# Eight first tiles of the final stage loaded in the expert stage, and eight more tiles kept on chip, in a three-stage graph kernel

## The chip, the cores and the metric

The kernel runs on one core of a Trainium2 chip. The metric is the time of one launch on the device in microseconds (us), measured on the chip. TensorE does the matrix products, VectorE, ScalarE and GpSimd the elementwise work, SyncE (SP) issues most of the DMA transfers; ScalarE (ACT in the rows) issues the stores of the result. GpSimd is POOL in the rows, VectorE DVE, TensorE PE, with PEld for its loads of weights. A q behind a name (SPq, POOLq) is the engine's queue, which works off waits, registers and branches.

## The reference, cut to what matters

There are 128 graphs of 128 nodes with 512 features each; x and adj are drawn at random.

```python
x = layernorm(x + attention(x, adj, adj, Wq, Wk, Wv, Wo))     # 16 heads, bias 2 * adj
# mixture of experts on the graph
scores = x.mean(axis=1) @ router_w + router_b
top1 = argmax(scores)                                          # one of 4 experts for each graph
out = einsum('bnm,bmk->bnk', adj, einsum('bnh,bhk->bnk', x, expert_w[top1]))
s, ss = sums of out and of out * out over the nodes and the graphs of each expert
y = (out - mean[top1]) * rsqrt(var[top1] + 1e-5) * gamma[top1] + beta[top1]
x = layernorm(x + relu(y))
```

The statistics of an expert need `out` of all its graphs, so `y` can be made only when the last `out` is there.

## The kernel before

One tile is one graph: 128 nodes on the partitions and 512 features in fp32, 262,144 bytes. The kernel has three stages, with a meeting of all engines between two of them.

The attention stage makes `x1`, the first normalised result, tile by tile and stores it to `x1_dram` (`x_scratch` in the rows). Its working tiles lie in `kept`, an array of 32 tiles in the chip's SBUF memory that the next stage fills.

The expert stage (`expert_phase`) takes 128 steps of one tile. SP loads x1 and the transposed adjacency four steps ahead into rings of four (`g_x1`, called `x1` in the function and `g_x` in the rows, and `adj_t`). TensorE forms adj @ x1 two steps ahead and then the product with the chosen expert's weights, each product as three passes over high and low parts. ScalarE copies the result (L752) and squares it (L754), and GpSimd adds both into the expert's sums (L835, L839). Every fourth tile (`is_kept`, place 2 of 4) is copied to `kept` and stays on chip. The other 96 go to a ring `g_out` and are stored by SP to `y_dram` (`y_scratch`, L663). The loop's body is written out for 8 steps and runs 15 times; the last 8 steps are written out after it with constants. Steps of such a written-out round are called peeled below.

The final stage (`norm_phase`) first makes the coefficients of each expert from the sums (TensorE, VectorE, ScalarE; `mul_row` is the last of them that GpSimd waits for, L1047). Then 128 steps follow in rings of 16 places: GpSimd multiplies the y tile with the expert's row (`scale`, L1101 to L1111), four tiles ahead of the rest; TensorE adds the expert's second row; VectorE takes the relu, adds x1 in place (L1058) and collects statistics; for every four tiles (a quad) GpSimd makes `rstd` (L1124) and `nb` (L1126); ScalarE applies them (L1144) and issues the store of the result (L1147). Before each scaling GpSimd's queue reads the number of the tile's expert into a register (L1102).

SP's queue sets the order of the loads. It first fills the ring of 16 (12 y tiles and 16 x1 tiles). In the loop it goes through the places in order: the y tile of the next round once TensorE has used the old one (L922), then the x1 tile once the old one's result has been stored (L925). y and x1 of a place count on one semaphore, so GpSimd's wait for a tile that isn't kept is a wait for both loads:

```python
                if is_kept(s):
                    pool.wait_ge(z_done, t + 1)
                    src = kept[:, bass.ds(i * QUADS + s // UNROLL, 1), :].rearrange("p a n -> p (a n)")
                else:
                    pool.wait_ge(tiles_in[s], i * 32 + 32)
                    src = y[:, s]
```

## Time and profile before

| What | Value |
|---|---|
| Median of three runs | 2771.8 us |
| Lowest and highest run | 2770.59 and 2773.67 us |
| The profiled execution's own time | 2769.72 us |
| Its span, first to last instruction | 2768.0 us |
| Busy share TensorE, VectorE, ScalarE, GpSimd | 96%, 69%, 55%, 46% |
| Attention, expert and final stage | to about 1985, to 2507, to 2768 us of the span |

The busy shares are means over three stages with different limits, so they tell little of the final stage. There one reads the stretches by themselves: how busy the DMA engines are in each, what an engine waits for there, and the distance from one quad to the next. A DMA share of 1.05 means all 16 DMA engines busy all the time.

### The profile page before, as it was taken

To read this page: it belongs to the slowest core of one execution; us is meant where nothing else is said; L and a number is where in the kernel's file an instruction comes from. 1 tells how busy PE (TensorE), PEld (TensorE's weight loads), DVE (VectorE), ACT (ScalarE), POOL (GpSimd) and SP (SyncE) were. 2 spreads that over 40 slices of the span, in tenths; PEclk is the share of its full clock that TensorE was granted. 3 is DMA by queue.
4 is the path that set the end of the run, shared out by engine and by line. 5 is a ranking of instruction groups with operands and counts; after the bars stand their busy time and mean duration, and the time that the engine had idled before them with its cause. 6 is when DMAs were issued, how large, how long until landed. Compare 5 with 4: busy or idle time off the path is not lost. (4 is left out here: it accounts for less than half of the span.)

```text
span 2768.0 us, 77846 instructions
## 1 busy us (share of the span) xinstructions
PE 2662.7 (96%) x22583; PEld 2264.7 (82%) x22584; DVE 1918.4 (69%) x8351; ACT 1514.5 (55%) x5391; POOL 1282.0 (46%) x1174
## 2 busy tenths in 40 slices
PE   8999999999999999999999999999799999997776
PEld 7898989898989888888888888888688888883232
DVE  6777777777777777777777777777733333335887
ACT  5565666666665656565656565656544444442444
POOL 2333334343434333334333433343366666666887
PEclk9999999999999999999999999999899999998998
DMA  4111111111111111111111111111234344445999
GB/s 147 62 53 54 53 62 53 54 53 62 53 54 53 62 54 53 57 58 58 49 58 56 58 49 64 51 57 52 75 123 141 131 138 131 136 134 197 396 405 352
DMA packets 169427, 277.32 MB, mean 100 GB/s; under 512 B 19378, under 2 KB 52146, under 8 KB 168882
## 3 DMA queue, kind: packets, MB, share of 16 engines
q1 hardware_dynamic: 150962, 243.36, 26.2%
q10 hardware_dynamic: 18432, 33.56, 3.2%
q8 instruction: 15, 0.25, 0.0%
q14 instruction: 18, 0.15, 0.0%
HBM read 184.57 MB, written 92.27 MB: 100 GB/s over the span
## 5 line engine op out<-in xcount | busy, mean ns | idle before, releaser
L553 POOL TENSOR_TENSOR kept<-kept,row_scale 128x512 f32<-128x512 f32 x512 | 533.4, 1042 | 1106.5 <-DVE row_scale L437 1096.4
L331 ACT ACTIVATE kept<-kept,neg_max 128x128 f32<-128x128 f32 x2048 | 796.0, 397 | 138.0 <-DVE neg_max L413 138.0
L413 DVE CUSTOM_DVE_ANT_0 kept<-att_bank,adj_nat 128x128 f32<-128x128 f32 x2048 | 442.6, 286 | 3.6 <-PE att_bank L212 1.6
L331 ACT ACTIVATION_READ_ACCUMULATOR kept<-kept,neg_max 128x1 f32 x2048 | 399.9, 195 | 0.0
L422 DVE TENSOR_REDUCE abs_max<-kept 128x4 f32<-128x512 f32 x512 | 349.2, 682 | 0.1
L191 PE MATMUL att_bank<-xt_hi,w_hi 128*128 128x256 f32 x2048 | 329.2, 283 | 11.2 <-DVE w_lo L390 11.2
L191 PE MATMUL att_bank<-xt_hi,w_lo 128*128 128x256 f32 x2048 | 329.7, 283 | 0.0
L191 PE MATMUL att_bank<-xt_lo,w_hi 128*128 128x256 f32 x2048 | 329.1, 283 | 0.0
L191 PEld LDWEIGHTS att_bank<-xt_hi,w_hi 128*128 128x128 f32 x2048 | 298.7, 191 | 30.7 <-issue 10.8
L364 ACT ACTIVATE kept<-att_bank 128x512 f32<-128x512 f32 x256 | 153.2, 599 | 279.8 <-PE att_bank L250 279.6
L191 PEld LDWEIGHTS att_bank<-xt_hi,w_lo 128*128 128x128 f32 x2048 | 282.7, 191 | 0.0
L191 PEld LDWEIGHTS att_bank<-xt_lo,w_hi 128*128 128x128 f32 x2048 | 282.4, 191 | 0.0
L479 DVE TENSOR_TENSOR o_lo<-att_bank,o_hi 128x512 fp32r<-128x512 f32 x128 | 88.5, 692 | 248.7 <-ACT o_hi L367 248.7
L250 PE MATMUL att_bank<-ident,kept 128*128 128x128 f32 x2048 | 248.1, 274 | 6.4 <-POOL kept L553 6.3
L463 DVE COPY kept<-att_bank 128x512 f32<-128x512 f32 x256 | 176.0, 688 | 94.9 <-PE att_bank L250 94.9
L250 PEld LDWEIGHTS att_bank<-ident,kept 128*128 128x128 f32 x2048 | 227.8, 141 | 9.1 <-POOL kept L553 5.4
L546 POOL TENSOR_TENSOR xt_lo<-kept,xt_hi 128x1024 fp32r<-128x1024 f32 x64 | 151.5, 2368 | 126.8 <-DVE xt_hi L475 117.0
L367 ACT ACTIVATE o_hi<-att_bank 128x512 fp32r<-128x512 f32 x128 | 76.5, 597 | 233.8 <-PE att_bank L258 233.8
L989 PE MATMUL ps_z<-n_y,ident 128*128 128x512 f32 x256 | 151.7, 676 | 52.3 <-POOL n_y L1109 47.5
L835 POOL TENSOR_TENSOR out_sum<-out_sum,g_out 128x512 f32 x96 | 123.7, 1289 | 134.9 <-ACT g_out L752 134.9
L1144 ACT ACTIVATE n_x<-n_x,n_nb,n_rstd 128x512 f32<-128x512 f32 x128 | 104.4, 815 | 131.3 <-POOL n_nb L1126 78.9
L752 ACT ACTIVATE g_out<-ps_o 128x512 f32<-128x512 f32 x96 | 57.4, 598 | 217.0 <-PE ps_o L702 217.0
(136 smaller groups left out, 5233.4 us busy)
## 6 DMA issues: line engine op xcount, KB each, us to landing
kept<-in_x_t SPq DMA_DIRECT2D x64, 512.0 KB, 3.5
kept<-in_x SPq DMA_DIRECT2D x128, 256.0 KB, 2.5
x_scratch<-kept SPq DMA_DIRECT2D x128, 256.0 KB, 2.0
g_x<-x_scratch SPq DMA_DIRECT2D x128, 256.0 KB, 2.7
n_x<-x_scratch SPq DMA_DIRECT2D x128, 256.0 KB, 6.2
out_x<-n_x ACTq DMA_DIRECT2D x128, 256.0 KB, 5.4
y_scratch<-g_out SPq DMA_DIRECT2D x96, 256.0 KB, 2.0
n_y<-y_scratch SPq DMA_DIRECT2D x96, 256.0 KB, 5.6
```

Source lines behind the costliest of these rows:

```text
L191: mm = pe.matmul(dst, w[:, which, k, c * P:(c + 1) * P], x[:, par, k, :], start=m == 0, stop=m == len(todo) - 1)
L250: mm = pe.transpose(bank[c][:, r * P:(r + 1) * P], probs[:, h * P:(h + 1) * P], ident[:, :])
L331: nc.scalar.activation(probs[:, h * P:(h + 1) * P], neg_s[:, h * P:(h + 1) * P], ACT.Exp, bias=neg_max[:, h:h + 1], scale=-1.0, accum_out= ...
L364: nc.scalar.activation(probs_t[:, c * D:(c + 1) * D], bank[c][:, :], ACT.Copy).then_inc(pt_odd, 1)
L413: nc.vector.tensor_tensor_reduce(neg_s[:, h * P:(h + 1) * P], bank[r][:, c * P:(c + 1) * P], adj_nat[:, s], -2.0, BIG, ALU.add, ALU.min, n ...
L422: nc.vector.tensor_reduce(abs_max[:, heads], neg_s[:, c * D:(c + 1) * D].rearrange("p (h m) -> p h m", h=HC), AX_X, ALU.max, apply_absolut ...
L463: nc.vector.tensor_copy(probs_t[:, c * D:(c + 1) * D], bank[c][:, :]).then_inc(pt_even, 1)
L546: nc.gpsimd.tensor_tensor(xt_lo[:, p], xt_stage[:, p], xt_hi[:, p].bitcast(F32), ALU.subtract).then_inc(xt_lo_done, 1)
L553: nc.gpsimd.tensor_tensor(part, part, by, ALU.mult).then_inc(probs_done, 1)
L835: nc.gpsimd.tensor_tensor(acc, acc, src, ALU.add).then_inc(sum_done, 1)
L989: pe.matmul(dst, ident[:, :], y[:, s], start=True, stop=False)
L1144: nc.scalar.activation(x1[:, s], x1[:, s], ACT.Identity, bias=nb[:, u, k:k + 1], scale=rstd[:, u, k:k + 1]).then_inc(out_done, 1)
```

## The change

Three things are changed together.

First, the first eight x1 tiles of the final stage are loaded while the expert stage ends: tiles 0 to 3 in steps 120 to 123 into a new array `early`, tiles 4 to 7 in steps 124 to 127 into the expert stage's ring `g_x1`, whose places are free by then. The two arrays become places 0 to 7 of the final stage's x1 ring (`x1_of`); places 8 to 15 remain in an array of their own.

Second, place 15 of every 16 tiles is kept too. Its eight tiles go to `w_stage`, the array through which weights were staged, so 88 instead of 96 tiles are stored and loaded again.

Third, to tell place 15 of 16 apart, the expert stage's loop body is written out for 16 steps and runs 7 times, with 16 peeled steps behind it. To make room, `g_out` has three places instead of four, the rows of `adj_t` are shorter, and the adjacency tiles and some small columns of the attention stage move into `kept`.

```diff
 BIG = 3.0e38
 UNROLL = 4
 KEPT_EVERY = UNROLL
+SPAN = 4 * UNROLL
+EARLY = 2 * UNROLL
 GROUP = 2
...
 def is_kept(s):
-    return s % KEPT_EVERY == KEPT_EVERY - 2
+    return s % KEPT_EVERY == KEPT_EVERY - 2 or s % SPAN == SPAN - 1
+
+
+def kept_tile(kept, more_kept, s, quad, span):
+
+    if s % SPAN == SPAN - 1:
+        return more_kept[:, bass.ds(span, 1), :].rearrange("p a n -> p (a n)")
+    return kept[:, bass.ds(quad, 1), :].rearrange("p a n -> p (a n)")
 def attention_phase(nc, io, W_hi, W_lo, w_stage, expert_w_in, ident, ones, g_x1, adj_t, hand_over, kept, pair,
...
         qk = [half[:, :, :].rearrange("p (w a) (b n) -> p w (a b) n", w=2, n=GN) for half in pair]
         xt_hi = sb("xt_hi", [P, 2, C, GN], F32R)
         xt_lo = sb("xt_lo", [P, 2, C, GN], F32R)
-        adj_nat = sb("adj_nat", [P, UNROLL, P])
+        adj_nat = kept[:, 30].rearrange("p (u n) -> p u n", u=UNROLL)
         o_hi = sb("o_hi", [P, C, P], F32R)
         o_lo = sb("o_lo", [P, C, P], F32R)
-        neg_max = sb("neg_max", [P, HEADS])
-        row_sum = sb("row_sum", [P, HEADS])
-        abs_max = sb("abs_max", [P, HEADS])
-        inv_sum = sb("inv_sum", [P, HEADS])
-        row_scale = sb("row_scale", [P, HEADS])
+        neg_max = kept[:, 31, 0 * HEADS:1 * HEADS]
+        row_sum = kept[:, 31, 1 * HEADS:2 * HEADS]
+        abs_max = kept[:, 31, 2 * HEADS:3 * HEADS]
+        inv_sum = kept[:, 31, 3 * HEADS:4 * HEADS]
+        row_scale = kept[:, 31, 4 * HEADS:5 * HEADS]
         stats = sb("stats", [P, 2, 6])
         mean_var = sb("mean_var", [P, 2, 2])
         var_eps = sb("var_eps", [P, 2])
...
     C = D // P
     HALF = C // 2
-    ROUNDS = 2
+    ROUNDS = SPAN // UNROLL
     with ExitStack() as ctx:
         def sb(name, shape, dt=F32):
             return ctx.enter_context(nc.sbuf_tensor(name, shape, dt))
...
         scores = sb("scores", [1, 2, 8])
         best = sb("best", [1, 2, 8])
         best_at = sb("best_at", [1, 2, 8], U32)
-        out = sb("g_out", [P, UNROLL, D])
+        out = sb("g_out", [P, UNROLL - 1, D])
         sq = sb("g_sq", [P, 2, D])
         ps_y = [ctx.enter_context(nc.psum_tensor(f"ps_y{i}", [P, 2, D], F32)) for i in range(2)]
...
                 for n in range(ROUNDS):
                     for s in range(UNROLL):
                         r = i * ROUNDS + n
-                        body(r * UNROLL + s, s, r, last, (n, s) == (ROUNDS - 1, UNROLL - 1))
+                        body(r * UNROLL + s, s, r, last, n * UNROLL + s, i)
             with eng.Fori(0, B // (ROUNDS * UNROLL) - 1) as i:
                 rounds(i, False)
             rounds(B // (ROUNDS * UNROLL) - 1, True)
+
+        def stores_ahead(s, place, span):
+
+            a_span = sum(not is_kept(n * UNROLL + s) for n in range(ROUNDS))
+            return span * a_span + sum(not is_kept(n * UNROLL + s) for n in range(place // UNROLL))
+
+        def out_of(s):
+            return out[:, s if s < KEPT_EVERY - 2 else s - 1]
         def exists(step, last, ahead):
             return not last or step + ahead < B
...
             sp.dma_start(router_w[:, :, :], io["router_w"].rearrange("(c p) e -> p c e", p=P)).then_inc(router_in, 16)
             sp.dma_start(router_b[:, :], io["router_b"].unsqueeze(0)).then_inc(router_in, 16)
-            def body(t, s, i, last, ends):
+            def body(t, s, i, last, place, span):
                 if exists(t, last, UNROLL):
                     sp.wait_ge(y_ps, t + 1)
                     load(t + UNROLL, s)
-                if not is_kept(s):
+                if not is_kept(place):
                     sp.wait_ge(out_done, t + 1)
-                    sp.dma_start(y_dram[t], out[:, s]).then_inc(out_stored[s], 16)
+                    sp.dma_start(y_dram[t], out_of(s)).then_inc(out_stored[s], 16)
+                if last and B - 2 * UNROLL <= t < B - UNROLL:
+                    sp.dma_start(early[:, s], x1_dram[s]).then_inc(early_in[s], 16)
+                if last and t >= B - UNROLL:
+                    sp.wait_ge(y_ps, t + 1)
+                    sp.dma_start(x1[:, s], x1_dram[UNROLL + s]).then_inc(early_in[UNROLL + s], 16)
             for_steps(sp, body)
             for s in range(UNROLL):
                 if not is_kept(s):
-                    sp.wait_ge(out_stored[s], 16 * (B // UNROLL + 1))
+                    sp.wait_ge(out_stored[s], 16 * (stores_ahead(s, 0, B // SPAN) + 1))
         @block.tensor
         def _(pe):
...
             for s in range(2):
                 y_high(s, s)
-            def body(t, s, i, last, ends):
+            def body(t, s, i, last, place, span):
                 if exists(t, last, 2):
                     y_high(t + 2, (s + 2) % UNROLL)
                 act.wait_ge(out_ps, t + 1)
-                if is_kept(s):
-                    dst = kept_tile(i)
+                if is_kept(place):
+                    dst = kept_tile(kept, more_kept, place, i, span)
                 else:
-                    act.wait_ge(out_stored[s], i * 16 + 16)
+                    act.wait_ge(out_stored[s], stores_ahead(s, place, span) * 16 + 16)
                     act.wait_ge(sum_done, t + 1)
-                    dst = out[:, s]
+                    dst = out_of(s)
                 nc.scalar.activation(dst, ps_o[s % 2][:, :], ACT.Copy).then_inc(out_done, 1)
                 act.wait_ge(sqsum_done, t + 1)
                 nc.scalar.activation(sq[:, s % 2], ps_o[s % 2][:, :], ACT.Square).then_inc(sq_done, 1)
...
             nc.gpsimd.memset(out_sq[:, :, :], 0.0).then_inc(filled, 1)
             pool.wait_ge(filled, 3)
-            def body(t, s, i, last, ends):
+            def body(t, s, i, last, place, span):
                 pool.wait_ge(expert_done, 2 * i + s // 2 + 2)
                 e = pool.value_load(expert_row[0:1, bass.ds(t, 1)], min_val=0, max_val=E - 1)
                 pool.wait_ge(out_done, t + 1)
                 pool.wait_ge(sum_done, t + UNROLL)
                 acc = out_sum[:, bass.ds(e, 1), :].rearrange("p a n -> p (a n)")
-                src = kept_tile(i) if is_kept(s) else out[:, s]
+                src = kept_tile(kept, more_kept, place, i, span) if is_kept(place) else out_of(s)
                 nc.gpsimd.tensor_tensor(acc, acc, src, ALU.add).then_inc(sum_done, 1)
                 pool.wait_ge(sq_done, t + 3)
                 pool.wait_ge(sqsum_done, t + 2)
...
         mul_row, add_row = sb("mul_row", [P, E, D]), sb("add_row", [P, E, D], F32R)
         pick = sb("pick", [P, P], F32R)
         y = sb("n_y", [P, RING, D])
-        x1 = sb("n_x1", [P, RING, D])
+        x1_late = sb("n_x1", [P, RING - EARLY, D])
+
+        def x1_of(s):
+            if s < EARLY:
+                return early[s // UNROLL][:, s % UNROLL]
+            return x1_late[:, s - EARLY]
+
         stats = sb("n_stats", [P, UNROLL, 6])
         mean_var = sb("n_mean_var", [P, UNROLL, 2])
         ve, nm = sb("n_ve", [P, QUADS, UNROLL]), sb("n_nm", [P, QUADS, UNROLL])
...
         col_hi_done, col_lo_done = sem("col_hi_done"), sem("col_lo_done")
         rows_ps, mul_done, add_done = sem("rows_ps"), sem("mul_done"), sem("add_done")
         into_done, quad_begun = sem("into_done"), sem("quad_begun")
-        tiles_in = [sem(f"n_tiles_in{i}") for i in range(RING)]
+        tiles_in = [*early_in, *(sem(f"n_tiles_in{i}") for i in range(EARLY, RING))]
         stored = [sem(f"stored{i}") for i in range(RING)]
         scaled_done, sum_ps, z_done = sem("scaled_done"), sem("n_sum_ps"), sem("z_done")
         picks = sem("picks")
...
                 sp.dma_start(y[:, s], y_dram[t]).then_inc(tiles_in[s], 16)
             def load_x1(t, s):
-                sp.dma_start(x1[:, s], x1_dram[t]).then_inc(tiles_in[s], 16)
+                sp.dma_start(x1_of(s), x1_dram[t]).then_inc(tiles_in[s], 16)
             for s in range(RING):
                 if not is_kept(s):
                     load_y(s, s)
-                load_x1(s, s)
+                if s >= EARLY:
+                    load_x1(s, s)
             def body(t, s, i, last):
                 if not last:
...
                 e = pool.value_load(expert_row[0:1, bass.ds(t, 1)], min_val=0, max_val=E - 1)
                 if is_kept(s):
                     pool.wait_ge(z_done, t + 1)
-                    src = kept[:, bass.ds(i * QUADS + s // UNROLL, 1), :].rearrange("p a n -> p (a n)")
+                    src = kept_tile(kept, more_kept, s, i * QUADS + s // UNROLL, i)
                 else:
                     pool.wait_ge(tiles_in[s], i * 32 + 32)
                     src = y[:, s]
...
         hand_over = e_hi_done, e_lo_done, g_x1_in, g_adj_in, ones_done
         kept = sb("kept", [P, B // KEPT_EVERY, D])
+        more_kept = w_stage[:, :, :, :].rearrange("p a c d -> p (a c) d")
+        early, early_in = sb("early_x1", [P, UNROLL, D]), [sem(f"early_in{i}") for i in range(EARLY)]
+        g_x1 = sb("g_x1", [P, UNROLL, D])
         out_sum, out_sq = sb("out_sum", [P, E, D]), sb("out_sq", [P, E, D])
         with ExitStack() as cut:
             W_hi = cut.enter_context(nc.sbuf_tensor("w_hi", [P, 4, C, D], F32R))
             W_lo = cut.enter_context(nc.sbuf_tensor("w_lo", [P, 4, C, D], F32R))
-            g_x1 = cut.enter_context(nc.sbuf_tensor("g_x1", [P, UNROLL, D], F32))
-            adj_t = cut.enter_context(nc.sbuf_tensor("adj_t", [P, UNROLL, P + P // 4], F32))
+            adj_t = cut.enter_context(nc.sbuf_tensor("adj_t", [P, UNROLL, P + 8], F32))
             attention_phase(nc, io, W_hi, W_lo, w_stage, expert_w_in, ident, ones, g_x1, adj_t, hand_over, kept, (out_sum, out_sq),
                             x1_dram, B, D)
-            expert_phase(nc, io, W_hi, W_lo, w_stage, expert_w_in, ones, expert_row, kept, out_sum, out_sq,
+            expert_phase(nc, io, W_hi, W_lo, w_stage, expert_w_in, ones, expert_row, kept, more_kept, out_sum, out_sq, early, early_in,
                          g_x1, adj_t, hand_over, x1_dram, y_dram, B, D, E)
-        norm_phase(nc, io, ident, ones, expert_row, kept, out_sum, out_sq, x1_dram, y_dram, out_dram, B, D, E)
+        norm_phase(nc, io, ident, ones, expert_row, kept, more_kept, out_sum, out_sq, (early, g_x1), early_in, x1_dram, y_dram, out_dram, B, D, E)
 def kernel(x, adj, L0_gnn_Wq, L0_gnn_Wk, L0_gnn_Wv, L0_gnn_Wo, L1_gnn_router_w, L1_gnn_router_b,
```

Where lines are left out, the functions' arguments and the uses of `x1_of` are changed in the same way.

SP's queue around the end of the expert stage: first as it was, from the last tile that is loaded to the second place of the final stage's ring (`n_y` and `n_x` are that stage's rings of y and x1).

```order
L652 DMA adj_t<-in_adj_t 128x128
L663 DMA y_scratch<-g_out 128x512 [waits out_done] x4
L584 UNCONDITIONAL_BRANCH [waits out_stored3,out_stored1,out_stored0]
L916 UNCONDITIONAL_BRANCH [waits barrier_Pool_Activation_PE_DVE_SP_release]
L918 DMA gamma<-in_gamma 128x16
L919 DMA beta<-in_beta 128x16
L922 DMA n_y<-y_scratch 128x512
L925 DMA n_x<-x_scratch 128x512
L922 DMA n_y<-y_scratch 128x512
L925 DMA n_x<-x_scratch 128x512 x2
L922 DMA n_y<-y_scratch 128x512
L925 DMA n_x<-x_scratch 128x512
```

And with the change, from the last of the loads into `early`:

```order
L679 DMA early_x<-x_scratch 128x512
L677 DMA y_scratch<-g_out 128x512 [waits out_done]
L682 DMA g_x<-x_scratch 128x512 [waits y_ps]
L677 DMA y_scratch<-g_out 128x512 [waits out_done]
L682 DMA g_x<-x_scratch 128x512 [waits y_ps] x3
L593 UNCONDITIONAL_BRANCH [waits out_stored3,out_stored1,out_stored0]
L941 UNCONDITIONAL_BRANCH [waits barrier_Pool_Activation_PE_DVE_SP_release]
L943 DMA gamma<-in_gamma 128x16
L944 DMA beta<-in_beta 128x16
L947 DMA n_y<-y_scratch 128x512 x7
L950 DMA n_x<-x_scratch 128x512
```

Four stores in a row have become two, each of which lets x1 loads for the final stage follow, and the final stage's first seven loads are y tiles alone.

GpSimd's queue in the final stage's loop, from the scaling of place 14 to the end of that quad, as it was:

```order
L1109 TENSOR_TENSOR n_y<-kept,mul_row 128x512
L1102 ISA
L1102 TENSOR_LOAD expert_row
L1102 ISA x2
L1109 ISA [waits n_tiles_in15]
L1109 TENSOR_TENSOR n_y<-n_y,mul_row 128x512
L1123 ISA
L1124 TENSOR_TENSOR n_rstd<-n_ve,half_u 128x4 [waits n_ve_done]
L1126 TENSOR_TENSOR n_nb<-n_nm,n_rstd 128x4 [waits n_rstd_done]
```

With the change:

```order
L1135 TENSOR_TENSOR n_y<-kept,mul_row 128x512
L1128 ISA
L1128 TENSOR_LOAD expert_row
L1128 ISA x2
L1130 REGISTER_ALU
L1135 ISA [waits z_done]
L1135 TENSOR_TENSOR n_y<-w_stage,mul_row 128x512
L1149 ISA
L1150 TENSOR_TENSOR n_rstd<-n_ve,half_u 128x4 [waits n_ve_done]
L1152 TENSOR_TENSOR n_nb<-n_nm,n_rstd 128x4 [waits n_rstd_done]
```

The scaling of place 15 reads `w_stage` and waits for `z_done`, a count of VectorE's, in place of the two loads of its place. One register operation is added.

SP's queue at the end of the final stage's loop body, as it was:

```order
L925 ISA [waits stored14]
L925 DMA n_x<-x_scratch 128x512
L922 ISA [waits n_sum_ps]
L922 DMA n_y<-y_scratch 128x512
L925 DMA n_x<-x_scratch 128x512 [waits stored15]
L908 REGISTER_ALU
L908 COMPARE_AND_BRANCH
```

With the change:

```order
L950 ISA [waits stored14]
L950 DMA n_x<-x_scratch 128x512
L950 ISA [waits stored15]
L950 DMA n_x<-x_scratch 128x512
L933 REGISTER_ALU
L933 COMPARE_AND_BRANCH
```

The y load of place 15 and its wait for TensorE are gone; the x1 load stays, with its wait for the store.

## Rows read from the trace of the kernel before

**Rows 1.** Windows of the final stage: busy of each engine, clock, DMA share, GB/s.

```profile
core 0: us, PE busy (x) PEld busy (x) DVE busy (x) ACT busy (x) POOL busy (x), PEclk, DMA share, GB/s
...
2508.00:2529.00 21.00, 15.06 (x55) 7.44 (x55) 10.02 (x22) 2.63 (x5) 5.54 (x7) 0.69 0.97 343
...
2529.00:2546.00 17.00, 12.80 (x30) 6.10 (x28) 10.68 (x23) 2.69 (x4) 13.80 (x13) 0.78 0.13 42
...
2555.00:2690.00 135.00, 104.42 (x231) 40.77 (x231) 113.62 (x268) 61.97 (x76) 116.89 (x116) 0.95 1.05 400
...
2690.00:2755.00 65.00, 49.72 (x110) 19.63 (x110) 54.03 (x128) 29.36 (x36) 56.09 (x55) 0.95 1.03 397
```

**Rows 2.** Timeline of SP's queue, seam and first ring.

```profile
2504.61 0.33 SPq L663 DMA_DIRECT2D y_scratch<-g_out  x1
...
2534.26 0.34 SPq L922 DMA_DIRECT2D n_y<-y_scratch  x1
...
2545.82 0.34 SPq L925 DMA_DIRECT2D n_x<-x_scratch  x1
```

**Rows 3.** Timeline of POOL, seam and final stage; brackets: idle before and releaser.

```profile
2505.98 1.26 POOL L839 TENSOR_TENSOR out_sq<-out_sq,g_sq 128x512 f32 x1
...
2530.19 2.48 POOL L1109 TENSOR_TENSOR n_y<-n_y,mul_row 128x512 f32<-128x512 f32 x2 [8.43 <-DVE mul_row L1047]
...
2541.41 1.01 POOL L1124 TENSOR_TENSOR n_rstd<-n_ve,half_u 128x4 f32<-128x4 f32 x1 [1.34 <-DVE n_ve L1076]
...
2555.14 1.02 POOL L1124 TENSOR_TENSOR n_rstd<-n_ve,half_u 128x4 f32<-128x4 f32 x1
...
2689.89 1.01 POOL L1124 TENSOR_TENSOR n_rstd<-n_ve,half_u 128x4 f32<-128x4 f32 x1
...
2695.92 1.28 POOL L1109 TENSOR_TENSOR n_y<-n_y,mul_row 128x512 f32<-128x512 f32 x1 [0.45 <-DMA n_x<-x_scratch]
...
2754.66 1.01 POOL L1124 TENSOR_TENSOR n_rstd<-n_ve,half_u 128x4 f32<-128x4 f32 x1
```

**Rows 4.** Waits, 2555 to 2690: total us, times, longest.

```profile
POOL n_y L1109 <- issue: 16.4, 20, 1.2
```

**Rows 5.** Line L1102, 2528:2550, then 2555:2690: ns min/median/max.

```profile
L1102 POOLq TENSOR_LOAD <-expert_row x13: 283/288/454, 2529.5 to 2549.3; - x13
...
L1102 POOLq TENSOR_LOAD <-expert_row x76: 282/317/1120, 2556.3 to 2686.5; - x76
```

**Rows 6.** The chain that ended last: start, us, what.

```profile
2696.35 5.48 DMA out_x<-n_x
2701.85 8.41 DMA n_x<-x_scratch
```

**Rows 7.** Timeline of ACT, expert stage: loop, then peeled round.

```profile
2105.20 0.60 ACT L752 ACTIVATE g_out<-ps_o 128x512 f32<-128x512 f32 x1 [2.32 <-PE ps_o L702]
...
2120.73 0.60 ACT L752 ACTIVATE g_out<-ps_o 128x512 f32<-128x512 f32 x1 [2.26 <-PE ps_o L702]
...
2136.32 0.60 ACT L752 ACTIVATE g_out<-ps_o 128x512 f32<-128x512 f32 x1 [2.32 <-PE ps_o L702]
...
2478.38 0.60 ACT L752 ACTIVATE g_out<-ps_o 128x512 f32<-128x512 f32 x1 [2.11 <-PE ps_o L702]
...
2493.63 0.60 ACT L752 ACTIVATE g_out<-ps_o 128x512 f32<-128x512 f32 x1 [1.99 <-PE ps_o L702]
```

**Rows 8.** Windows: four attention steps, then eight expert steps.

```profile
1008.38:1069.68 61.30, 61.30 (x612) 54.89 (x616) 47.34 (x218) 36.89 (x152) 23.43 (x23) 1.00 0.18 56
2105.20:2136.32 31.12, 31.12 (x171) 26.51 (x170) 11.54 (x56) 13.12 (x24) 20.29 (x16) 1.00 0.42 134
```

**Rows 9.** Lines L116, L639, branches of TensorE's queue: ns min/median/max.

```profile
L116 PEldq COMPARE_BRANCH  x2: 207/208/208, 1017.3 to 1078.6; - x2
...
L639 PEldq COMPARE_BRANCH  x4: 207/208/208, 2099.1 to 2192.5; - x4
```

**Rows 10.** The page's DMA issues: KB each, median us to landing.

```profile
gamma<-in_gamma SPq DMA_DIRECT2D x1, 8.0 KB, 1.6
```

More of the change, by code:

```diff
@@ L572, in _, with expert_phase @@
             for_steps(pool, body)
-def expert_phase(nc, io, W_hi, W_lo, w_stage, expert_w_in, ones, expert_row, kept, out_sum, out_sq,
+def expert_phase(nc, io, W_hi, W_lo, w_stage, expert_w_in, ones, expert_row, kept, more_kept, out_sum, out_sq, early, early_in,
                  x1, adj_t, hand_over, x1_dram, y_dram, B, D, E):
@@ L594, in y_of @@
             return both[:, :, :, 0:P], both[:, :, :, P:P + 1]
-        def kept_tile(r):
-            return kept[:, bass.ds(r, 1), :].rearrange("p a n -> p (a n)")
         def halves_of(ring, s):
@@ L806, in _, with body @@
             route(0, 0)
-            def body(t, s, i, last, ends):
+            def body(t, s, i, last, place, span):
                 if exists(t, last, 2):
@@ L826, in _, with body @@
             pool.wait_ge(filled, 3)
-            def body(t, s, i, last, ends):
+            def body(t, s, i, last, place, span):
                 pool.wait_ge(expert_done, 2 * i + s // 2 + 2)
@@ L841, in _, with norm_phase @@
             for_steps(pool, body)
-def norm_phase(nc, io, ident, ones, expert_row, kept, out_sum, out_sq, x1_dram, y_dram, out_dram, B, D, E):
+def norm_phase(nc, io, ident, ones, expert_row, kept, more_kept, out_sum, out_sq, early, early_in, x1_dram, y_dram, out_dram, B, D, E):
     C = D // P
@@ L1057, in body @@
                     dve.wait_ge(tiles_in[place], (i + 1) * (16 if is_kept(place) else 32))
-                    nc.vector.scalar_tensor_tensor(out=x1[:, place], in0=ps_z[place % SUMS][:, :], scalar=0.0,
-                                                   in1=x1[:, place], op0=ALU.max,
+                    nc.vector.scalar_tensor_tensor(out=x1_of(place), in0=ps_z[place % SUMS][:, :], scalar=0.0,
+                                                   in1=x1_of(place), op0=ALU.max,
                                                    op1=ALU.add).then_inc(z_done, 1)
@@ L1062, in body @@
                     dve.wait_ge(z_done, n + 1 + RING)
-                    nc.vector.bn_stats(stats[:, place % UNROLL], x1[:, place]).then_inc(stats_done, 1)
+                    nc.vector.bn_stats(stats[:, place % UNROLL], x1_of(place)).then_inc(stats_done, 1)
                 if s % UNROLL == UNROLL - 1:
@@ L1143, in body @@
                 act.wait_ge(nb_done, i * QUADS + u + 1)
-                nc.scalar.activation(x1[:, s], x1[:, s], ACT.Identity, bias=nb[:, u, k:k + 1],
+                nc.scalar.activation(x1_of(s), x1_of(s), ACT.Identity, bias=nb[:, u, k:k + 1],
                                      scale=rstd[:, u, k:k + 1]).then_inc(out_done, 1)
                 act.wait_ge(out_done, t + 1)
-                act.dma_start(out_dram[t], x1[:, s]).then_inc(stored[s], 16)
+                act.dma_start(out_dram[t], x1_of(s)).then_inc(stored[s], 16)
             for_steps(act, body)
```

## Prediction

> **What bounds the kernel now.** I read the final stage first, because the change aims at it, then its seam with the expert stage, then the expert loop, whose code also changes.
>
> The windows of the final stage [rows 1] show four stretches. From 2508 to 2529 the first ring is loaded, at a DMA share of 0.97. From 2529 to 2546 the DMA engines have almost nothing to do (0.13, 42 GB/s). From 2555 to 2690 their share is 1.05 at 400 GB/s, and to 2755 it is 1.03: there they are full. The reader should see the hole between two full stretches. SP's queue [rows 2] tells why it is there: the first y tile of the second ring is issued at 2534.26, the next command is the first x1 tile of that ring, it waits for the store of place 0, and goes out only at 2545.82; all later y loads stand behind it.
>
> GpSimd's timeline [rows 3] gives the pace. The `rstd` of a quad (four tiles) starts at 2541.41 for the first, 2689.89 for the 22nd and 2754.66 for the 31st. That is 21 intervals of 7.07 us (148.48/21), then 9 of 7.20 us (64.77/9), and 7.108 us over all 30 (213.25/30). Against that stand two floors. The DMA engines move 11 tiles of 262,144 bytes in a quad (4 x1, 3 y, 4 stores); at 400 to 405 GB/s a tile takes about 0.65 us, so a quad takes 7.1 to 7.2. GpSimd's own work is nearly as long: between 2555 and 2690 its idle time before the scalings is put down to "issue" [rows 4], 16.4 us in 20 pieces, and the list of waits of that stretch has none of GpSimd for a DMA; these are the moments in which its queue reads the expert number for the next tile. So up to 2690 it is GpSimd that sets the pace, with the DMA engines full beside it but not late; after 2690 the loads are late as well, the first such wait being 0.45 us at 2695.92 [rows 3]. The chain there goes store, load, scaling: 5.48 us for the store and 8.41 for the load of x1 that waited for it [rows 6]. The two bounds lie within 2% of each other, and that decides this case.
>
> In the expert stage TensorE is busy without a gap (31.12 of 31.12 us) at a DMA share of 0.42 [rows 8].
>
> **The change, part by part.**
>
> *Eight x1 tiles loaded early.* They leave the first ring's stretch, 2508 to 2529. At 0.65 us they are 5.2 us of transfers. But who waits for that ring? GpSimd's first scaling starts at 2530.19 after 8.43 us idle, released by VectorE's `mul_row` and not by a load [rows 3]; then comes the hole. Transfers taken out ahead of a hole make the hole longer. The ring is still 16 deep, and the load of a next x1 tile still waits for the store of the same place. I cost this at nothing. The cover is the coefficient work up to 2529; without it the price is the 5.2 us. In the expert stage the loads add 2.1 MB to eight steps, 67 GB/s beside 134 at a share of 0.42 [rows 8], and SP needs about 0.34 us to issue one [rows 2] in steps of 3.9 us. The last four wait for y products already made two steps before. Nothing.
>
> *The seam.* The last tile is no longer stored, so SP leaves the stage sooner. Before, its last store was issued at 2504.61 [rows 2]; GpSimd's last sum of squares runs from 2505.98 to 2507.24 [rows 3], is unchanged, and is what the engines meet behind. Nothing.
>
> *Eight y tiles kept.* The eight stores leave the expert stage, where they were hidden. Of the eight loads one was in the first ring (nothing, as above) and seven in the full stretches: 7 x 0.65 = 4.5 us of DMA work. A ring round falls from 44 transfers to 43, a quad's floor on average from 7.1 to 6.95 us. This is the uncertain term. If the DMA engines alone bounded the stage, all 4.5 us would be gained. If GpSimd's own pace of the first 21 quads holds, the late quads go from 7.20 to 7.07 and the gain is 213.25 - 30 x 7.07 = 1.15 us. I take 1.15: the rows nearest to it are the 21 quads in which no load was waited for, and they say that GpSimd needs 7.07 us whatever the loads do. The end between is a GpSimd that itself gets faster when the DMA engines are less full. Its read of the expert number took 288 ns at the median (454 at most) when they were nearly idle and 317 (1120 at most) when they were full [rows 5], and its first two quads, partly in the hole, took 6.87 us each (2541.41 to 2555.14) [rows 3]. They will be 99% full after the change (27.9 of 28.3 us a round), so little of this comes back. At place 15 GpSimd now waits, in place of both loads, until the sum of the tile sixteen before has been used, which is long past; its other instructions there are the same but for one register operation.
>
> *Loop of 16 steps in the expert stage.* There are 6 jumps back instead of 14, and the last round, written out with constants, is 16 steps instead of 8. ACT's copies [rows 7] give the step: four steps inside the loop's body 15.53 us (2105.20 to 2120.73), four that hold the jump 15.59, four of the written-out round 15.25 (2478.38 to 2493.63). Eight more written-out steps save (15.53 + 15.59) - 2 x 15.25 = 0.62 us. That counts one of the eight jumps; seven more at 0.06 are 0.42. Together 1.04 us. Below, nothing at all; above, eight times the 0.21 us that a jump takes TensorE's queue [rows 9], with the 0.62: 2.3 us.
>
> Does a longer body make a jump dearer? TensorE's jump took 207 to 208 ns both in the attention loop, whose four steps hold 612 matmuls, and in the expert loop, whose eight hold 171 [rows 8, 9]. Sixteen steps hold some 342, less than a body that already jumps at that price.
>
> The Trainium skill, "Runtime: NRT & Kernel Launch", section "Instruction fetch mechanics", speaks against the longer body: it says that a taken jump to code outside a small window of fetched pages must wait until that page has been fetched. By that rule the six jumps left would each cost a fetch and the 1.04 us would turn into a loss; the rows just named do not show such a cost for a body that is longer still.
>
> *Places of tiles in memory.* The adjacency tiles and the small columns of the attention stage lie inside `kept`, the rows of `adj_t` are 136 elements instead of 160. Instructions, shapes and waits are the same. Nothing; a price here would fall on about 2000 us of work, and no row shows one.
>
> **Sum.** 0 + 0 - 1.15 - 1.04 = -2.2 us. On the profiled execution's own time of 2769.72 us (2768.0 of span) that is 2767.5. This execution lies 2.1 us under the median of the runs, 2771.8; the forecast for a median is 2769.6.
>
> **The rivals.**
>
> *The DMA engines bound the whole stage.* For it: they are full from 2555 to 2755, and the mean quad, 7.108 us, is just their floor. Against it: no wait for a load before 2690. It gives -4.5 - 1.04 = -5.6: 2766.2, just at the bound of what can be told from no change, 0.2% (5.5 us).
>
> *All 16 tiles count, the eight early ones too.* 16 x 0.65 + 1.04 = 11.4 us: 2760.4. It needs something in the first 38 us of the stage that waits for the ring; rows 3 name `mul_row` instead.
>
> *Slower: the longer loop's jumps.* If the code of a 16-step body has to be fetched again at each of six jumps, at the 1.6 us in which the smallest load of the page landed [rows 10], the loss is 9.6 us: 2771.8 - 1.15 + 9.6 - 0.62 = 2779.6. It decides from 1.2 us a jump on ((5.5 + 1.15 + 0.62)/6). Against it stands the attention loop.
>
> *The change does nothing that shows.* If GpSimd's pace is 7.1 in the late quads too and the loop's gain is nil, 2771.8.
>
> **How the numbers follow.** The forecast, a small gain, 0.52; the full gain of the loads 0.27; all sixteen 0.08; the slower loop 0.08; nothing 0.05. The predicted time is 2769.6. Half of the second case falls past 0.2%, and a little of the first: faster 0.27, slower 0.08, same 0.65. The range of 8 in 10 reaches to the second case, less half the spread of the runs shown (1.5 us), hence 2765.0, and upwards to no gain with some spread, 2773.0.
>
> **What would show it.** In the changed profile: the hole after the first ring begins some 6 us earlier and still ends near 2546 less the expert stage's gain. The quads take 7.05 to 7.1 us to the end with no wait of GpSimd for a DMA, and the DMA share stays near full. Quads near 6.95 would say that the DMA engines were the bound; an earlier first scaling, that the ring was waited for. Eight expert steps should take 31.06 us in the loop (four without a jump 15.53) and 30.5 written out. A jump of TensorE's queue above 0.21 us, or expert steps longer at the jump, would prove the slower rival.

## The result, and the profile after

The changed kernel takes 2780.89 us at the median (2778.98 to 2782.72, 9 runs) against 2771.76 (2770.59 to 2773.67, 9 runs): ratio 1.0032, interval 1.0024 to 1.0041. It is slower by some 9 us, outside the predicted range of 2765.0 to 2773.0.

The first look goes to the places at which the change aimed. The windows of the final stage after the change, the answers to [rows 1] and, in the fifth row, to the attention steps of [rows 8]:

```profile
core 0: us, PE busy (x) PEld busy (x) DVE busy (x) ACT busy (x) POOL busy (x), PEclk, DMA share, GB/s
2520.00:2541.00 21.00, 15.07 (x53) 7.11 (x52) 9.47 (x19) 2.63 (x5) 5.33 (x5) 0.66 0.66 238
2541.00:2558.00 17.00, 12.62 (x32) 6.21 (x30) 10.61 (x23) 2.36 (x4) 13.48 (x12) 0.78 0.11 32
2567.00:2702.00 135.00, 103.67 (x228) 40.45 (x226) 117.80 (x267) 61.87 (x76) 116.31 (x115) 0.95 1.05 393
2702.00:2767.00 65.00, 51.20 (x113) 20.09 (x113) 55.65 (x126) 29.31 (x36) 56.33 (x56) 0.95 1.01 381
1013.67:1075.27 61.60, 61.60 (x612) 54.93 (x616) 47.31 (x218) 36.84 (x152) 23.41 (x23) 1.00 0.17 55
```

The first ring now keeps the DMA engines 0.66 busy instead of 0.97; the hole (0.11 instead of 0.13) and the full stretches (1.05 and 1.01 instead of 1.05 and 1.03) are nearly as they were. The fifth row is the surprise: the same 612 matmuls, four steps at granted clock 1.00 and without a gap, take 61.60 us instead of 61.30, in the attention stage, where the prediction had costed the change at nothing.

SP's queue and GpSimd in the final stage, timeline rows that answer to [rows 2, 3]:

```profile
2546.64 0.34 SPq L947 DMA_DIRECT2D n_y<-y_scratch  x1
2558.12 0.34 SPq L950 DMA_DIRECT2D early_x<-x_scratch  x1
```

```profile
2517.71 1.26 POOL L858 TENSOR_TENSOR out_sq<-out_sq,g_sq 128x512 f32 x1
...
2542.57 2.48 POOL L1135 TENSOR_TENSOR n_y<-n_y,mul_row 128x512 f32<-128x512 f32 x2 [8.42 <-DVE mul_row L1073]
...
2553.74 1.01 POOL L1150 TENSOR_TENSOR n_rstd<-n_ve,half_u 128x4 f32<-128x4 f32 x1 [1.30 <-DVE n_ve L1102]
...
2702.75 1.00 POOL L1150 TENSOR_TENSOR n_rstd<-n_ve,half_u 128x4 f32<-128x4 f32 x1
...
2766.64 1.01 POOL L1150 TENSOR_TENSOR n_rstd<-n_ve,half_u 128x4 f32<-128x4 f32 x1
```

The first scaling still waits 8.42 us for `mul_row`, and the second ring's first x1 load is issued 11.48 us after its y load (11.56 before). GpSimd's waits from 2567 to 2767:

```profile
POOL n_y L1135 <- issue: 24.6, 28, 1.4
POOL n_rstd L1150 <- DVE n_ve L1102: 0.2, 1, 0.2
```

The waits for loads are gone; from 2555 to 2755 before they were 2.2 us in 7 pieces, beside 22.2 us put down to "issue". But "issue" has grown to 24.6 us, so GpSimd idles as long as before, and all 30 quads took 212.90 us (2766.64 - 2553.74) against 213.25.

The loss doesn't lie in the quads, then. ScalarE's `o_hi` copy comes once in an attention step; its first two rows and its last in that stage, then the first, 112th and last copy of the expert stage, before:

```profile
42.79 0.60 ACT L367 ACTIVATE o_hi<-att_bank 128x512 fp32r<-128x512 f32 x1 [3.02 <-PE att_bank L258]
58.12 0.60 ACT L367 ACTIVATE o_hi<-att_bank 128x512 fp32r<-128x512 f32 x1 [1.83 <-PE att_bank L258]
...
1987.28 0.60 ACT L367 ACTIVATE o_hi<-att_bank 128x512 fp32r<-128x512 f32 x1 [1.21 <-PE att_bank L258]
...
2011.84 0.60 ACT L752 ACTIVATE g_out<-ps_o 128x512 f32<-128x512 f32 x1 [5.43 <-PE ps_o L702]
...
2443.46 0.60 ACT L752 ACTIVATE g_out<-ps_o 128x512 f32<-128x512 f32 x1 [2.21 <-PE ps_o L702]
...
2503.99 0.60 ACT L752 ACTIVATE g_out<-ps_o 128x512 f32<-128x512 f32 x1 [1.72 <-PE ps_o L702]
```

And after, with two copies of place 15 in the loop between (2144.80 and 2207.02, of which more below):

```profile
43.54 0.60 ACT L376 ACTIVATE o_hi<-att_bank 128x512 fp32r<-128x512 f32 x1 [3.02 <-PE att_bank L267]
...
1998.02 0.60 ACT L376 ACTIVATE o_hi<-att_bank 128x512 fp32r<-128x512 f32 x1 [1.30 <-PE att_bank L267]
...
2023.99 0.60 ACT L771 ACTIVATE g_out<-ps_o 128x512 f32<-128x512 f32 x1 [5.19 <-PE ps_o L721]
...
2144.80 0.60 ACT L771 ACTIVATE w_stage<-ps_o 128x512 f32 x1 [2.31 <-PE ps_o L721]
2207.02 0.60 ACT L771 ACTIVATE w_stage<-ps_o 128x512 f32 x1 [2.31 <-PE ps_o L721]
...
2455.90 0.60 ACT L771 ACTIVATE w_stage<-ps_o 128x512 f32 x1 [2.31 <-PE ps_o L721]
...
2515.72 0.60 ACT L771 ACTIVATE w_stage<-ps_o 128x512 f32<-128x512 f32 x1 [1.72 <-PE ps_o L721]
```

127 attention steps take 1954.48 us instead of 1944.49 (+9.99). The start of the kernel adds 0.75 and the passage to the expert stage 1.41 (25.97 against 24.56). The first 111 expert steps are +0.29, the last 16 (all written out after the change, eight of them before) -0.71, the passage to the first `rstd` +0.60, the quads -0.35, and what follows the 31st `rstd` +0.62 (13.96 against 13.34). That is the whole 12.6 us between the two spans, 2768.0 and 2780.6. These two profiled executions lie further apart than the medians (9.1 us). The attention steps alone account for a loss of that size; the two passages vary by more than +1.41 and +0.60 without a change of theirs: over the 14 profiles of kernels that keep the expert and final stages as they were, the first takes 21.49 to 26.68 us and the second 37.31 to 38.69.

Within a step, TensorE's timeline tells which products are slower. Rows of four matmuls each (the moving operand first, then the one that is loaded as weights), before:

```profile
1012.27 1.10 PE L308 MATMUL att_bank<-w_hi,o_hi 128*128 128x512 f32 x4
1013.21 1.07 PE L308 MATMUL att_bank<-w_lo,o_hi 128*128 128x512 f32 x4
1014.11 1.07 PE L308 MATMUL att_bank<-w_hi,o_lo 128*128 128x512 f32 x4
1015.02 0.64 PE L191 MATMUL att_bank<-xt_hi,w_hi 128*128 128x256 f32 x4
```

And after:

```profile
1017.58 1.09 PE L317 MATMUL att_bank<-w_hi,o_hi 128*128 128x512 f32 x4
1018.50 1.10 PE L317 MATMUL att_bank<-w_lo,o_hi 128*128 128x512 f32 x4
1019.44 1.09 PE L317 MATMUL att_bank<-w_hi,o_lo 128*128 128x512 f32 x4
1020.37 0.64 PE L200 MATMUL att_bank<-xt_hi,w_hi 128*128 128x256 f32 x4
```

From start to start, the first group takes 0.92 us instead of 0.94, the second 0.94 instead of 0.90, the third 0.93 instead of 0.91: together 2.79 us instead of 2.75. The rest of the step's loss is spread over other products in pieces of 0.01 to 0.02 us, the last digit of such rows. These products were not touched by the change; what moved is where their operands lie.

The kernels' layout, in bytes of a partition: shortening the four rows of `adj_t` by 24 elements each moves all that lies behind it 384 bytes towards the weights `w_hi` and `w_lo`; `g_x1` (8,192 bytes), which lay between, has moved ahead of them. From `w_hi` to `xt_hi` it was 76,288 bytes before (a multiple of 256) and is 67,712 (128 more than one). For `xt_lo`, `o_hi` and `o_lo` it is the same: multiples of 256 before, 128 more than one after.

### The profile page after: what moved, and what is told of

It is laid out like the page before. It is cut to its first block and busy times, and to the rows that moved or that the text cites. A ratio compares the mean times of both kernels' runs of the same rounds, so it can differ in the third digit from the quotient of the medians.

```text
span 2780.6 us, 77620 instructions
## 1 busy us (share of the span) xinstructions
PE 2676.5 (96%) x22583; PEld 2268.1 (82%) x22584; DVE 1924.8 (69%) x8351; ACT 1510.1 (54%) x5391; POOL 1282.4 (46%) x1174
## 5 line engine op out<-in xcount | busy, mean ns | idle before, releaser
L562 POOL TENSOR_TENSOR kept<-kept 128x512 f32<-128x512 f32 x512 | 532.8, 1041 | 1117.7 <-DVE kept L446 1112.5
L340 ACT ACTIVATE kept<-kept 128x128 f32<-128x128 f32 x2048 | 794.0, 393 | 138.7 <-DVE kept L422 138.7
L422 DVE CUSTOM_DVE_ANT_0 kept<-att_bank,kept 128x128 f32<-128x128 f32 x2048 | 442.5, 286 | 4.5 <-PE att_bank L221 2.4
L340 ACT ACTIVATION_READ_ACCUMULATOR kept<-kept 128x1 f32 x2048 | 392.7, 192 | 0.0
L431 DVE TENSOR_REDUCE kept<-kept 128x4 f32<-128x512 f32 x512 | 349.1, 682 | 0.1
L783 DVE TENSOR_TENSOR products<-ps_y,router_w 128x16 f32<-128x16 f32 x128 | 22.8, 178 | 219.0 <-PE ps_y L699 218.6
L209 PE MATMUL att_bank<-w_lo,xt_hi 128*128 128x512 f32 x512 | 174.2, 422 | 0.0
L854 POOL TENSOR_TENSOR out_sum<-out_sum,g_out 128x512 f32 x88 | 114.8, 1304 | 122.3 <-ACT g_out L771 122.3
```

What stands on the lines that cost most here:

```text
L209: mm = pe.matmul(bank[b][:, :], x[:, par, k, j * P:(j + 1) * P], w[:, V, k, :], start=m == 0, stop=m == len(todo) - 1)
L340: nc.scalar.activation(probs[:, h * P:(h + 1) * P], neg_s[:, h * P:(h + 1) * P], ACT.Exp, bias=neg_max[:, h:h + 1], scale=-1.0, accum_out= ...
L422: nc.vector.tensor_tensor_reduce(neg_s[:, h * P:(h + 1) * P], bank[r][:, c * P:(c + 1) * P], adj_nat[:, s], -2.0, BIG, ALU.add, ALU.min, n ...
L431: nc.vector.tensor_reduce(abs_max[:, heads], neg_s[:, c * D:(c + 1) * D].rearrange("p (h m) -> p h m", h=HC), AX_X, ALU.max, apply_absolut ...
L562: nc.gpsimd.tensor_tensor(part, part, by, ALU.mult).then_inc(probs_done, 1)
L854: nc.gpsimd.tensor_tensor(acc, acc, src, ALU.add).then_inc(sum_done, 1)
```

## The experiments

Theory P: the places of `xt_hi`, `xt_lo`, `o_hi` and `o_lo` cost the time. Theory K: the small tiles that were moved into `kept` do. Beside them: the early loads, and the longer loop. Steps are the distance of `o_hi` copies in the profile, at the median: 15.33 us in the kernel before, 15.40 in the changed one. Ratios are to the kernel before, run beside each kernel (medians 2771.21 to 2772.87).

**The parts of the change one by one.** First the small tiles alone in the kernel before, with unused arrays in their old places so that nothing else moves:

```diff
-        adj_nat = sb("adj_nat", [P, UNROLL, P])
+        adj_nat = kept[:, 30].rearrange("p (u n) -> p u n", u=UNROLL)
+        sb("pad_adj", [P, UNROLL, P])
```

and the same for the five columns.

> The kernel before, with the attention stage's adjacency tiles and five small columns inside kept as in the change, and unused arrays in their old places, so that every other array keeps its address. Theory K (the small tiles in kept slow the attention stage): its steps go from 15.33 to 15.40 us and the time to about 2781 us. Theory P (the changed addresses of the other arrays do): steps of 15.33 us and 2772 us, no difference from before.

Measured 2771.95 us, ratio 1.0000 [0.9991, 1.0010], step 15.33: theory K falls. Then the reverse, the changed kernel with these tiles in arrays of their own again (the lines above with + and - exchanged, without the unused arrays):

> The changed kernel, with the adjacency tiles and the five columns in arrays of their own again, behind the other arrays of the attention stage, which keep the changed kernel's addresses. Theory K: attention steps of 15.33 us and 2771 to 2772 us in all. Theory P: steps of 15.40 us and about 2780 us.

Measured 2780.37, ratio 1.0030 [1.0019, 1.0041], step 15.40. It agrees. The changed kernel without early loads:

```diff
-                if last and B - 2 * UNROLL <= t < B - UNROLL:
-                    sp.dma_start(early[:, s], x1_dram[s]).then_inc(early_in[s], 16)
...
-                if s >= EARLY:
-                    load_x1(s, s)
+                load_x1(s, s)
```

> The changed kernel without the early loads: all 16 x1 tiles of the first ring are loaded at the start of the final stage, into the same places. My step that the early loads are worth nothing: 2781 us, no difference from the changed kernel (at most 0.5 us), first scaling at the same distance from the stage's start. The rival that they count: some 5 us slower, 2786 us.

Measured 2779.7, ratio 1.0028 [1.0017, 1.0039]. The early loads are neither a gain that shows nor the loss: the 2786 us of the rival (ratio 1.005) lies outside the interval. The other way round, place 15 kept and the loop of 16 in the kernel before, whose arrays stay where they are (two lines of the edit):

```diff
+    return s % KEPT_EVERY == KEPT_EVERY - 2 or s % SPAN == SPAN - 1
...
+    ROUNDS = SPAN // UNROLL
```

> The kernel before, with place 15 kept in the weights' staging array and the loop of 16 steps, without early loads and with every array at its address of before. Both theories: attention steps of 15.33 us. If GpSimd sets the final stage's pace, 2769.6 to 2771 us (ratio 0.9992 to 0.9997); if the DMA engines do, 2766 to 2767 us (ratio 0.998).

Measured 2770.39, ratio 0.9995 [0.9986, 1.0004], step 15.33: no loss in the loop. A small gain is likely, but the interval doesn't prove it. It does exclude the ratio of 0.998 expected if the DMA engines alone bound the final stage.

**The places.** The changed kernel with `adj_t` as long as before, so that all behind it moves back by 384 bytes:

```diff
-            adj_t = cut.enter_context(nc.sbuf_tensor("adj_t", [P, UNROLL, P + 8], F32))
+            adj_t = cut.enter_context(nc.sbuf_tensor("adj_t", [P, UNROLL, P + P // 4], F32))
```

> The changed kernel with rows of adj_t of 160 elements again: every array behind it lies 384 bytes further on, at the same offset within 2048 bytes as in the kernel before (128 for o_hi and o_lo). Theory O (the offset of o_hi and o_lo decides the speed of the last product's matmuls): attention steps of 15.33 us and 2770 to 2771 us. Theory W (the addresses of the weight arrays, which lie 16,384 bytes further on, decide): steps of 15.40 us and 2780 us.

Measured 2770.43, ratio 0.9994 [0.9985, 1.0003], step 15.33: the whole loss is gone, with all else of the change in place. This is the decisive run for theory P. Theory W of the expectations, by which the weights' own addresses count, falls here too. Moving only `o_hi` and `o_lo`, in the changed kernel by 384 bytes (shown) and in the kernel before to their changed places (1440 elements, 5760 bytes):

```diff
+        sb("pad_o", [P, 96])
         o_hi = sb("o_hi", [P, C, P], F32R)
```

> The changed kernel with 384 unused bytes ahead of o_hi, so that o_hi, o_lo and the small arrays behind them alone move, to an offset of 128 within 2048 bytes. Theory O: attention steps of 15.33 us, 2770 to 2771 us. Theory W: 15.40 us, 2780 us. If the xt arrays' offset matters in its place: 15.40 us here and 15.33 us with adj_t of 160.

> The kernel before with 5760 unused bytes ahead of o_hi, so that o_hi and o_lo lie at the changed kernel's addresses and everything ahead of them at its own. Theory O: attention steps of 15.40 us and 2781 us. Theory W: 15.33 us and 2772 us.

Measured 2774.26, ratio 1.0009 [0.9999, 1.0019], step 15.37, and 2775.48, ratio 1.0015 [1.0006, 1.0024], step 15.36. Theory O (the `o` arrays alone) would have made them 15.33 and 15.40. In the profiles, 4.9 of the 9.99 us in 127 steps remain with the `o` arrays put back, and 4.3 arise with them alone moved: they cause about one half, the `xt` arrays the other. The whole times are too coarse for this split; the interval of the first includes no loss at all. Moving the weights by 8192 bytes (`g_x1` allocated ahead of the sums):

> The kernel before with the ring g_x1 ahead of out_sum, so that the sums and both weight arrays lie 8192 bytes further on and all arrays behind them at their addresses of before. Theory O: attention steps of 15.33 us, 2772 us. Theory W: another step than 15.33 us, up to 15.40 us and 2781 us.

Measured 2771.56, ratio 0.9999 [0.9989, 1.0009]: no effect, but 8192 is a multiple of any period in question.

**Which distance.** In the kernel before, an unused array ahead of `xt_hi`, of 128, 384, 1664 and 1920 bytes:

```diff
+        sb("ahead_of_xt", [P, 32])
         xt_hi = sb("xt_hi", [P, 2, C, GN], F32R)
```

> The kernel before, computing everything, with 128 unused bytes per partition ahead of xt_hi, so that xt_hi, xt_lo, o_hi and o_lo lie 128 bytes further on (256 instead of 128 bytes past a multiple of 512 and of 2048). Theory H (the place within 512 bytes, the width of one 128-column block, counts): same remainder by 512 as in the changed kernel, so the attention step is 15.40 us instead of 15.33 and the time about 2781. Theory T (the place within 2048 bytes, the width of one row of 512, counts): the remainder is neither kernel's, nothing is fixed; 15.33 is as likely as 15.40. If the place of these arrays does nothing, 15.33 and 2772 in all four kernels of this call.

> The same with 384 unused bytes: the arrays start at a multiple of 512, 512 bytes past a multiple of 2048. Theory H: the same step as with 1920 bytes, whatever it is. Theory T: may differ from that.

> The same with 1664 unused bytes: the arrays start 1792 bytes past a multiple of 2048, as in the changed kernel, and nothing else of the change is there. Theories H and T both: step 15.40 us, 126 steps longer by 0.075 each, so about 2781. If the step stays at 15.33, it is not the remainder by 2048 of these four arrays, and the explanation by their places has to be found in distances to other arrays.

> The same with 1920 unused bytes: the arrays start at a multiple of 2048. Theory H: the same step as with 384 bytes. Theory T: may differ. A step below 15.33 would show that the kernel before was not at the best place either, and give a version faster than both.

All four are slow: 2783.28, 2781.33, 2781.97 and 2782.57, ratios 1.0036, 1.0029, 1.0036 and 1.0034 (the lowest interval 1.0016 to 1.0042), steps 15.40. An unused array of 128 bytes reproduces the loss of the whole change. All four sizes are odd multiples of 128, whatever remainder by 512 or 2048 they leave (theories H and T), and up to here the arrays' own place and their distance to the weights could not be told apart. So next both are moved by 128 bytes, then the weights alone (with `adj_t` 128 bytes shorter), then the arrays by 256 and 512:

```diff
+            cut.enter_context(nc.sbuf_tensor("ahead_of_w", [P, 32], F32))
             W_hi = cut.enter_context(nc.sbuf_tensor("w_hi", [P, 4, C, D], F32R))
```

> The kernel before, computing everything, with 128 unused bytes ahead of w_hi, so that the weights, g_x1, adj_t and the four attention arrays all lie 128 bytes further on: the attention arrays are where they were in before_xt_128 (step 15.40), but the distance between them and the weights is that of the kernel before. Theory D (the distance to the weights, by some power of two, counts, because the weights stream through TensorE while the attention arrays are loaded): step back at 15.33, time 2772. Theory A (the arrays' own place counts): 15.40 and 2782.

> The kernel before with 128 unused bytes ahead of w_hi and the rows of adj_t shortened by 8 elements (128 bytes in all), so that the weights lie 128 bytes further on and the attention arrays exactly where they were. Theory D: step 15.40 and 2782 although the attention arrays have not moved. Theory A: 15.33 and 2772.

> The kernel before with 256 unused bytes ahead of xt_hi: 128 bytes past a multiple of 256, but 384 past one of 512. If a period of 256 bytes or less counts, step 15.33; if 512 or more, 15.40 (2782).

> The kernel before with 512 unused bytes ahead of xt_hi: 128 bytes past a multiple of 512, but 640 past one of 2048. If a period of 512 bytes or less counts, step 15.33 and 2772; if 2048, 15.40 and 2782.

Measured 2772.03, ratio 1.0002 [0.9991, 1.0013]; 2780.96, ratio 1.0031 [1.0017, 1.0045]; 2772.64, ratio 1.0002 [0.9991, 1.0013]; 2771.78, ratio 0.9998 [0.9986, 1.0009]. Theory D holds and A falls: with weights and arrays moved together nothing is lost, and with the weights moved alone 8 us are (2780.96 against 2772.87, step 15.40), though no attention array stands elsewhere than before. `g_x1` and `adj_t` move in both kernels, so they are not the cause. A distance that stays a multiple of 256 costs nothing. Last, 64 and 192 bytes ahead of `xt_hi`:

> The kernel before with 64 unused bytes ahead of xt_hi, everything computed: the distance from the weights to the attention arrays is 64 bytes past a multiple of 256, between the short step (0) and the long one (128). If the step is 15.33, the distance may be off by up to 64 bytes at no cost; 15.40 says that only the multiple of 256 itself (or less than 64 off) is free; about 15.36 says that the cost grows with the distance; below 15.33, that 0 was not the best place and there is a version faster than both.

> The same with 192 unused bytes: 64 short of a multiple of 256. If only the size of the deviation from a multiple counts, the same as with 64 bytes; if the order of the two addresses counts, the other value. The step is 15.33 or 15.40, the time 2772 or 2782.

Measured 2772.62, ratio 1.0001 [0.9990, 1.0013], step 15.32; and, against the expectation, 2750.50 (two runs, 2750.46 and 2750.55), ratio 0.9924 [0.9895, 0.9953]. 192 unused bytes make the kernel before 21 us faster than it was, and 30 us faster than the changed one. Groups of matmuls from 300 to 1900 us (busy us, mean ns of one), of the kernel before, then of before_xt_64, then of before_xt_192:

```profile
L191 PE MATMUL att_bank<-xt_hi,w_lo 128*128 128x256 f32 x1664 | 267.6, 283 | 0.0
...
L308 PE MATMUL att_bank<-w_lo,o_hi 128*128 128x512 f32 x416 | 111.2, 389 | 0.0
```

```profile
L192 PE MATMUL att_bank<-xt_hi,w_lo 128*128 128x256 f32 x1668 | 264.1, 279 | 0.0
...
L309 PE MATMUL att_bank<-w_lo,o_hi 128*128 128x512 f32 x416 | 113.9, 396 | 0.0
```

```profile
L192 PE MATMUL att_bank<-xt_hi,w_lo 128*128 128x256 f32 x1684 | 263.4, 279 | 0.0
...
L309 PE MATMUL att_bank<-w_lo,o_hi 128*128 128x512 f32 x424 | 114.4, 392 | 0.0
```

With 64 bytes the products that stream `xt` get faster (283 to 279 ns) and these two that stream the weights slower (389 to 396), and the two cancel. The ends of matmuls are modelled, so starts are the better measure. Mean us from start to start in 83 or 84 steps of each profile between 500 and 1800 us, by the bytes past a multiple of 256 (the transposes, 1.66 to 1.67 us in all four, are left out):

| Stretch of a step | 0 (before) | 64 | 128 (changed) | 192 |
|---|---|---|---|---|
| Three groups that stream the weights past `o` | 2.75 | 2.81 | 2.80 | 2.76 |
| Twelve groups that stream `xt` | 5.75 | 5.65 | 5.75 | 5.57 |
| The groups that stream the weights past `xt`, with what lies between | 5.16 | 5.20 | 5.18 | 5.17 |
| Whole step | 15.33 | 15.32 | 15.40 | 15.16 |

At 128 the products that stream the weights lose and those that stream `xt` gain nothing; at 192 those that stream `xt` gain 0.18 us and the others lose next to nothing. Two steps of before_xt_192 take 30.32 us (907.36 to 937.68 in its `o_hi` copies) against 30.65 before (901.09 to 931.74), and all 127 take 1924.53 us against 1944.49: 20.0 of the 21 us.

## Why the prediction was wrong, by its own steps

**The step that failed** is "Places of tiles in memory … Nothing; a price here would fall on about 2000 us of work, and no row shows one". The work on which a price would fall was named rightly, the price was not nothing: 15.40 instead of 15.33 us a step, 9.99 us in the 127 steps of the profiles, against a forecast of -2.2 for everything together. No row of the kernel before could show a price, since every row had the same distances; the absence of a row was taken for a zero. None of the four rivals held this case either. Shown is that the time of an attention step follows the distance in bytes between the weight arrays and the `xt` and `o` arrays, the operands that stream and that are loaded in the same matmuls. The distance alone doesn't give one rate for all: in the kernel before, where every distance is a multiple of 256, the three groups shown take 0.94, 0.90 and 0.91 us. Why the distance counts stays open: no run looks into how the two operands are read. The Trainium skill, "SBUF — State Buffer", section "Who interferes with whom", gives TensorE two read ports, for the moving operand and for the weights, and calls them independent. By that alone no distance would cost anything; before_w_128 (+8 us from 128 bytes) disagrees.

**Early loads: nothing.** Right as far as the runs tell. Without them the ratio is 1.0028 [1.0017, 1.0039], with them 1.0032 [1.0024, 1.0041], and `mul_row` releases the first scaling as before. **The seam: nothing.** Near enough: +0.60 us between the last expert copy and the first `rstd`, within the spread of that passage.

**Eight kept y tiles: -1.15.** Right in kind; the size is probably too small. The two profiles compared above show only -0.35. Over the profiles of all kernels here, the 30 quads take 211.57 us in the mean of the six kernels with 11 y tiles in a ring (210.06 to 212.90) and 213.83 in that of the 14 with 12 (213.25 to 214.59): -2.26 us, between the forecast and the -4.5 of the rival in which the DMA engines alone bound the stage. A quad is 7.05 us, not 6.95, and in five of the six GpSimd waits for no load in the last 200 us of quads (in changed_small_back 0.5 us in 2 pieces). That speaks for GpSimd's pace as the bound that is left; it isn't proved, since the DMA share stays at 1.01 to 1.05 beside it and no run changed one of the two alone.

**Loop of 16: -1.04.** Half right. The eight more written-out steps gave -0.71 (forecast -0.62). The seven saved jumps gave nothing: 16 steps in the loop take 62.22 us after (2144.80 to 2207.02 in the copies shown above) and took two times 31.12 before [rows 7], and the 111 steps of the loop's stretch are +0.29.

The difference between four steps with and without a jump in [rows 7] (0.06) was thus not the jump's price.

**The slower rival,** the longer loop's jumps, named the right sign and the wrong cause. TensorE's jumps after the change (ns min, median, max):

```profile
L645 PEldq COMPARE_BRANCH  x7: 76/208/217, 2080.5 to 2453.8; - x7
```

The median is that of [rows 9], and kept15_loop16, which has these jumps, loses nothing. No run shows here a fetch after a taken jump as the Trainium skill, "Runtime: NRT & Kernel Launch", section "Instruction fetch mechanics", would have it.

With the places put right, the change is worth what changed_adj160 shows: 2770.43 against 2772.07. That is close to the forecast of 2769.6, but the interval, 0.9985 to 1.0003, includes no gain at all. The changed kernel with 192 bytes of distance was not run.

## What to carry to other kernels

An edit that only moves or shortens an array also moves every array allocated behind it, and that can cost or give more than the edit itself: compare the addresses of both kernels, above all of the operands of a stage in which TensorE has no gap. If a stage that the edit doesn't touch changes its step, hold the addresses fixed with unused arrays before looking for any other cause. And as no trace of one layout shows what another would cost, try some distances between the streamed and the loaded operand (here 0, 64, 128 and 192 bytes past a multiple of 256) as one tunes a tile size.

## What the runs showed of the hardware

- At granted clock 1.00, three groups of four 128x512 matmuls that stream the weights past `o` take 0.94, 0.90 and 0.91 us from start to start where the arrays lie a multiple of 256 bytes from the weights, and 0.92, 0.94 and 0.93 us where they lie 128 past one.
- The distance counts modulo 256 as far as tried: +256 and +512 cost nothing that shows, +128, +384, +1664 and +1920 each 9 to 11 us of 2772.
- It isn't symmetric: +64 costs nothing in the sum, +192 gives 21 us. Products that stream `xt` and those that stream the weights answer differently: at +192 the first take 5.57 us of a step instead of 5.75, at +128 they stay at 5.75 while the second lose.
- Eight loads of 262,144 bytes taken out of a stretch in which the DMA engines were 0.97 busy gave no gain that shows: the stretch fell to 0.66, the hole behind it stayed (0.11), and the first scaling still waited 8.42 us for `mul_row`.
